# Value blocks side by side behind the whole fold, with scores and mixing in other PSUM banks

## What is computed

```python
x_c = einsum('bct,bcd->bdt', x, W[condition])                 # 128 samples, 32 tokens, 512
q_c = hidden @ Wq_c.T + bq_c                                  # 192 wide
q   = (q_c @ Wq_up.T + bq_up) -> 32 heads of 192
kv  = hidden @ Wkv_c.T + bkv_c                                # 64 latent + 64 rope
k_nope, v = (kv[..., :64] @ Wkv_up.T + bkv_up) -> 32 heads
scores = einsum('bhqd,bhkd->bhqk', q, [k_nope, k_rope]) / sqrt(192)
attn = softmax(scores, axis=-1)
o    = einsum('bhqk,bhkv->bhqv', attn, v)
out  = einsum('bhsv,Hv->bsH', o, Wo) + bo
x = x + out;  x = x + ffn(conv(x))
```

## Time and profile before

| | us |
|---|---|
| median of 3 runs | 777.69 |
| lowest, highest | 776.83, 778.36 |
| the profiled execution | 776.39 |
| its span, first to last instruction | 774.6 |
| TensorE matmuls busy in it | 752.9 |
| VectorE, ScalarE, GpSimd busy in it | 619.5, 379.4, 200.4 |

### The profile page before, as it was taken

One profiled execution on the slowest core, in us unless ns is written; L12 is line 12 of the kernel. 1 busy time (PEld: TensorE's weight loads), 2 busy tenths in 40 slices (PEclk: granted clock), 3 DMA queues, 4 the chain that ended last, 5 costly groups with the idle time before them and its releaser, 6 DMA issues.

```text
span 774.6 us, 18461 instructions
## 1 busy us (share of the span) xinstructions
PE 752.9 (97%) x7757; PEld 597.5 (77%) x7757; DVE 619.5 (80%) x1109; ACT 379.4 (49%) x675; POOL 200.4 (26%) x203
## 2 busy tenths in 40 slices
PE   9999999999999999999999999999997799999996
PEld 6777686778668767868686687778676599999996
DVE  5676899989998786777768776877889588888887
ACT  2475546546563765555454646555664322222221
POOL 4002020020002010271200000000041488888871
PEclk9999999999999999999999999999999999999999
DMA  9910010010001001001300010002207158888861
GB/s 226 243 54 5 2 58 3 1 60 2 2 2 59 2 1 29 1 3 16 84 2 2 2 55 2 1 2 58 83 2 199 55 120 216 206 204 204 203 136 69
DMA packets 42738, 51.74 MB, mean 67 GB/s; under 512 B 7024, under 2 KB 29600, under 8 KB 42656
## 3 DMA queue, kind: packets, MB, share of 16 engines
q1 hardware_dynamic: 40384, 49.87, 25.9%
q0 software_dynamic: 1056, 0.49, 0.3%
q10 hardware_dynamic: 1216, 0.19, 0.2%
HBM read 41.91 MB, written 8.63 MB: 65 GB/s over the span
## 4 chain that ended last, share of the span: by engine, by line
PE 93%; DVE 3%; ACT 2%; issue 1%; POOL 0%; DVEq 0%
PE ps L730 34%; PE ps L598 9%; PE ps L599 8%; PE ps L600 8%; PE ps L774 7%; PE ps L797 4%; PE ps L1075 4%; PE ps L1076 4%; PE ps L616 4%; PE ps L1044 2%; PE ps L693 1%; DVE z_low L1435 1%; PE ps L1032 1%; PE ps L1034 1%; PE ps L1033 1%
## 5 line engine op out<-in xcount | busy, mean ns | idle before, releaser
L1176 ACT ACTIVATE qt<-ps,m_bias 128x512 f32<-128x512 f32 x228 | 145.7, 686 | 98.7 <-PE ps L730 98.7
L730 PE MATMUL ps<-q_high,m_high 64*128 64x512 f32 x768 | 154.5, 398 | 2.0 <-ACT qt L1176 1.3
L730 PE MATMUL ps<-q_high,m_low 64*128 64x512 f32 x768 | 150.6, 388 | 0.0
L730 PE MATMUL ps<-q_low,m_high 64*128 64x512 f32 x768 | 108.2, 386 | 0.0
L1435 DVE TENSOR_TENSOR z_low<-ps,z_high 128x512 fp32r<-128x512 f32 x128 | 79.7, 683 | 17.2 <-ACT z_high L1194 15.1
L730 PEld LDWEIGHTS ps<-q_high,m_high 64*128 64x128 f32 x768 | 72.4, 184 | 24.2 <-issue 7.9
L528 POOL TENSOR_TENSOR o_sum<-o_part,o_part 128x512 f32<-128x512 f32 x7 | 9.1, 1303 | 291.8 <-ACT o_part L1204 291.8
L730 PEld LDWEIGHTS ps<-q_low,m_high 64*128 64x128 f32 x768 | 72.5, 184 | 14.9
L730 PEld LDWEIGHTS ps<-q_high,m_low 64*128 64x128 f32 x768 | 72.5, 184 | 13.8
L1194 ACT CAST z_high<-ps 128x512 fp32r<-128x512 f32 x128 | 66.7, 597 | 18.7 <-PE ps L797 9.5
L1181 ACT ACTIVATE sc<-sc 128x512 f32<-128x512 f32 x60 | 37.3, 632 | 46.6 <-DVE sc L1420 43.1
(11 more groups left out here) (292 smaller groups left out, 1647.3 us busy)
## 6 DMA issues: line engine op xcount, KB each, us to landing
x_in<-in_x SPq DMA_DIRECT2D x16, 512.0 KB, 3.6
x_s<-in_x SPq DMA_DIRECT2D x32, 256.0 KB, 5.5
out<-res SPq DMA_DIRECT2D x31, 256.0 KB, 3.3
toep_high<-taps_scratch SPq DMA_DIRECT2D x32, 192.0 KB, 4.4
toep_low<-taps_scratch SPq DMA_DIRECT2D x32, 192.0 KB, 4.9
toep_far<-taps_scratch SPq DMA_DIRECT2D x32, 64.0 KB, 5.6
wq_nope<-in_L_attn_Wq_up SPq DMA_DIRECT2D x2, 768.0 KB, 10.7
wq_nope<-in_L_attn_Wq_up SPq DMA_DIRECT2D x1, 1536.0 KB, 17.5
```

The costliest lines, as they stand in the source:

```text
L730: mm = pe.matmul(ps[:, fold_bank(u, j) + e, :], weights[rows, (GH * g + j) // 2, c, :], moving[c][rows, :], start=start, stop=stop)
L1176: act.activation(qt[:, j, :], ps[:, fold_bank(u, j) + j % 2, :], ACT.Identity, bias=m_bias[:, h:h + 1]).then_inc(s["qt_done"], 1)
```

## The change

The two value blocks now follow each other, behind all 16 heads of the fold, in units 1 to 14. Block 1 of units up to 13 goes to BT, BT + 1, BS, BS + 1, which are the fold's banks, so it waits for all heads to be taken (qt_done and qt_last), and no longer for z_low. Scores go to BZ, BZ + 1, BX, BT instead of BS, BS + 1, BX, BT: in units from 1 the four groups wait for z_low 1, 2, 3 and 5 of the unit before, where the first two waited for none; in unit 0 the first group waits for the weights' low parts (fold_done 6 and wvT_done 4), where the third waited for wvT_done 4. Mixing goes to BT + 1, BS (even) and BS + 1, BZ (odd). The waits of turn_latent, tap_products and turned_ffn(0) are turned to counters of scores taken, as their banks are now held by scores. ScalarE takes the four banks of block 0 in one go behind head 14, VectorE takes head 15 ahead of the first z_low.

```diff
-    ZBANK = ((BZ, BZ + 1, BX, BO), (BT, BT + 1, BZ, BZ + 1))
+    ZBANK = ((BZ, BZ + 1, BX, BO), (BT, BT + 1, BS, BS + 1))
-    SBANK = (BS, BS + 1, BX, BT)
+    SBANK = (BZ, BZ + 1, BX, BT)
-    MIX_BANK = lambda i, e: (BS + e if i % 2 else BT + e if i == 0 else (BT + 1, BZ)[e])
+    MIX_BANK = lambda i, e: (BS + e if i == 1 else BT + e if i == 0 else ((BT + 1, BS), (BS + 1, BZ))[i % 2][e])
...
                 elif i >= 2:
-                    pe.wait_ge(s["s_taken"], 4 * (i - 2) + 2)
+                    pe.wait_ge(s["zl_done"], 8 * (i - 2))
+                    pe.wait_ge(s["s_taken"], 4 * (i - 2) + 1)
...
                 if k == 0:
                     pe.wait_ge(s["fold_done"], QUADS - 2)
-                else:
-                    pe.wait_ge(s["zl_done"], 16 * k)
+                pe.wait_ge(s["s_taken"], 8 * k + 2)
...
-                if n == 2:
-                    if u == 0:
-                        pe.wait_ge(s["wvT_done"], 4)
-                    else:
-                        pe.wait_ge(s["zl_done"], 8 * (u - 1) + 3)
-                if n == 3 and u >= 1:
-                    pe.wait_ge(s["zl_done"], 8 * (u - 1) + 5)
+                if u >= 1:
+                    pe.wait_ge(s["zl_done"], 8 * (u - 1) + (1, 2, 3, 5)[n])
+                elif n == 0:
+                    pe.wait_ge(s["fold_done"], QUADS - 2)
+                    pe.wait_ge(s["wvT_done"], 4)
...
-                        pe.wait_ge(s["qt_done"], qt_count(v, GH - 2))
-                        pe.wait_ge(s["qt_last"], 2 * v - 1)
-                        pe.wait_ge(s["zl_done"], 8 * u + 2)
+                        pe.wait_ge(s["qt_done"], qt_count(v, GH))
+                        pe.wait_ge(s["qt_last"], 2 * v)
...
                     fold(u, 8, 16)
-                    values(0, 0)
-                    scores(1, 0)
-                    scores(1, 1)
-                    values(0, 1)
-                    scores(1, 2)
-                    scores(1, 3)
                 else:
-                    fold(u, 0, 14)
-                    values(u - 1, 0)
-                    fold(u, 14, 16)
-                    values(u - 1, 1)
-                    for n in range(4):
-                        scores(u, n)
+                    fold(u, 0, 16)
+                values(u - 1, 0)
+                values(u - 1, 1)
+                for n in range(4):
+                    scores(u, n)
...
-                    values(u - 1, 0, 0, 3)
                     fold(u, 14, 16)
-                    values(u - 1, 0, 3, 4)
+                    values(u - 1, 0, 0, 4)
...
                 late_head(u, GH - 3)
-                if u == 1:
-                    late_head(u, GH - 1)
-                    values(0, 0, 0, 4)
-                else:
-                    values(u - 1, 0, 0, 2)
-                    late_head(u, GH - 1)
-                    values(u - 1, 0, 2, 4)
+                late_head(u, GH - 1)
+                values(u - 1, 0, 0, 4)
```

More of the change, by code:

```diff
@@ L874, in tap_products @@
                 pe.wait_ge(s["gf_ready"], 1)
-                if n == 0:
-                    pe.wait_ge(s["zl_done"], 64)
-                else:
-                    pe.wait_ge(s["s_taken"], 4 * 8 + 3)
+                pe.wait_ge(s["s_taken"], 4 * 8 + (1, 3)[n])
                 for h in range(16 * n, 16 * n + 16):
@@ L886, in turned_ffn @@
                 if k == 0:
-                    pe.wait_ge(s["zl_done"], 8 * (LAST - 1))
+                    pe.wait_ge(s["s_taken"], 4 * (LAST - 1) + 1)
                 if k == 1:
```

## The result

| | before | after |
|---|---|---|
| median, us (20 runs each) | 775.81 | 779.06 |
| lowest, highest | 773.93, 778.36 | 775.64, 780.67 |
| the profiled execution, us | 776.39 | 780.49 |
| its span, us | 774.6 | 778.7 |
| mean granted TensorE clock in it | 0.998 | 0.993 |

The ratio is 1.0037, 95% interval 1.0025 to 1.0049: slower by 0.37%, some 2.9 us (the plain difference of the two medians is 3.3). The median lies within 0.3 us of the forecast and inside its range, but the kernel before came out 1.9 us lower in this larger set of runs than in the three that the forecast started from. So the difference is 2.9 us and not 1.1, and that the median came so near is luck: the start was taken 1.9 us too high and the difference 1.8 us too small, and the two cancel. The outcome is "slower by over 0.2%", which had 41%, not "within 0.2%", which had 46% and was the forecast.

A forecast was written before the change was run, and what follows sets the result against it. TensorE's stream was taken to bound the kernel. The terms +2.0 - 0.88 + 1.24 - 1.04 - 0.21 gave +1.1 us; 777.69 stood 1.3 under the forecast of 778.8 us, range 776.8 to 781.0.

The forecast's parts named there:

- What bounds the kernel: TensorE, busy 752.9 of 774.6 us; time moves only where its own stream gets shorter or longer.
- The ordinary unit: Units 2 to 8, 10 to 13, start of block 0 (V) to output: 8.28 us, 0.18 longer each, +2.0 together.
- Unit 1: Its end, where scores were split around block 1 and waited three times: -0.88 us.
- unit 0: Its first scores group newly waits for all four value weights, wvT_done 4: +1.24 us.
- unit 14: Its end, 8.49 us because of unpacked weights, goes to 8.28 as the z chain starts later: -0.21 us.
- Block 1's wait for both late heads: Block 1's new wait at unit ends is covered by block 0's 1.13 us, with 0.1 us over.
- Unit 9: Its end, 9.32 us from ScalarE's late z_high, goes to 8.28: -1.04 us, or 0 if the stall stays.
- Rival 4: A stall like that in unit 9 stays on the ScalarE and VectorE path: +2.1 us, 779.8; 15%.
- Rival 3: Fourth (and second) score groups wait as z_low runs slower, 0.17 us in 13 units: +3.3 us, 781.0; 20%.
- Rival 2: Drains at tiling changes decide, first z_low not late, every unit's end at 7.87 us: -4.2 us, 773.5; 12%.
- The LAST unit's code is the same: From the LAST unit to the end nothing changes: 0 us.
- What follows in a unit: Scores are taken from 0.5 us behind the output's start; turned latents and second mixing stay covered, no new wait.

The follow-up runs named there:

- the longer wait: The changed kernel with unit ends' first scores group waiting for the second z_low instead of the first; 788.41 us, 1.0136 of before.
- filled: Matmuls without a reader added in TensorE's waits of the tail, to either kernel: 775.64 and 774.43 us for before, 777.22 and 776.92 for changed.
- the padded kernel: The kernel before with seven idle matmuls of 512 columns ahead of unit 3's fold; 778.94 us against 778.03, ratio 1.0008.

## Why the prediction was right, and where it missed

**What bounds the kernel** was right: TensorE's stream, and the first z_low as the thing that ends the wait in each unit. **The ordinary unit** came out step by step: the pair 2.0 us (2.04), V + 1.24 and V + 1.86 unchanged, scores at V + 2.67 (2.67), output at V + 6.27 (6.24). The blocks' matmuls end at V + 2.19, so TensorE stands 0.51 (forecast 0.41, with the blocks ending at V + 2.26 at the latest); the sum is the same, since the z_low ends the wait in either case. The waiting is shown by making it longer (0.60 more gave 0.60 more).

**Unit 1** (-0.85 for -0.88), **unit 0** (+1.21 for +1.24) and **unit 14** (-0.21) were right; for the first two the experiments took or gave back just that. Block 1's wait for both late heads was covered, except in unit 1, where block 1 stands 0.67 us behind block 0's loads. The scores would have waited for the z_low until V + 2.67 in any case and start at V + 2.79, so this costs 0.1 (V to output 6.36 for 6.27).

**Unit 9, the step that failed within the sum.** I wrote that its stall "would be spent before anything needs ScalarE" and took -1.04. But it isn't tied to ScalarE's place in the stream, nor to ScalarE. In the changed kernel (weight loads, then ScalarE, then SyncE):

```profile
369.57 2.57 PEld L795 LDWEIGHTS ps<-pT,ctok 32*64 32x64 f32 x128 [0.35 <-issue]
372.31 0.14 PEld L772 LDWEIGHTS ps<-qt,kv 128*32 128x32 f32 x5 [0.17 <-issue]
...
376.33 0.19 PEld L598 LDWEIGHTS ps<-z_high,wvT_high 128*128 128x128 f32 x1 [0.84 <-DVE z_low L1421]
```

```profile
370.82 4.25 ACT L1181 CAST z_high<-ps 128x512 fp32r<-128x512 f32 x8 [0.45 <-PE ps L795]
```

```profile
365.55 2.30 SPq L380 DMA_DIRECT2D taps_scratch<-o_sum  x3
```

Here ScalarE is on time, at V + 1.25, but TensorE's own 128 loads stretch from 1.95 to 2.57, and its scores' stretch is longer too. Before, it was ScalarE that was late: in all six profiles with the old order the loads of block 0 take their 0.96, and z_high starts at V + 1.46 to V + 2.33 instead of 1.24, with block 1's loads halted as well in the kernel before (1.22 instead of 0.96). In the six with the new order z_high starts at V + 1.25 to 1.61, and TensorE's loads are halted. In the seventh, with the longer wait, both are late (z_high at V + 2.04, loads in three pieces). V to output was 6.76 to 7.53 in these six, where the ordinary units have 6.27, and 8.69 to 9.32 in the old six, where they have 8.11. So the stall hits unit 9 in either order, on ScalarE's side in the old one and mostly on TensorE's in the new, and moving ScalarE's work didn't spend it. Rival 4 was right in this, and its +2.1 is the nearest to what was measured, though it put the stall in ScalarE's and VectorE's chain. So unit 9 changed by -0.56, +0.09 and +0.34 in three pairs of profiles instead of -1.04. In each profile three stores of the convolution's taps are issued by SyncE 2.4 to 4.6 us ahead of V, loads of x behind them, and the DMA engines are 0.8 busy or more in a part of unit 9's end (0.92 from 370 to 372 us here). That these transfers cause the stall is argued from the coincidence; no kernel moved them, and it stays **open**.

**Rival 3** did not occur: eight z_low take 4.87, which is 0.60 from one to the next, and the fourth score group didn't wait. **Rival 2** needed scores that don't wait for z_low; they wait 0.51 us in each ordinary unit.

**The tail, the step that failed outside the sum.** "The LAST unit's code is the same" was taken to mean that its time is. Its instructions are; their clock isn't. In the first pair 2.6 of 4.1 us arose there. That this is the clock and not the changed banks is shown by the tails above: filled, both kernels take the same, and unfilled their length goes with the time at the lower level. The shift alone didn't bring it in the padded kernel, and over the runs the loss is in both kernels. Of the 20 runs of the changed kernel two had a mean clock of 1.0 (775.64 and 776.12) and the other eighteen 0.991 to 0.996 (777.85 to 780.67). Between the filled kernels the change costs 1.6 and 2.5 us on two chips, 0.2 to 0.3%; between the kernels as they are, 2.9 and 2.3 by the ratios. From the first fold to V of unit LAST, the three profiles with the whole old order take 544.2 to 544.7 us and the four with the whole new one 546.3 to 547.1, 2.3 apart in the mean. So the forecast's +1.1 was low by some 1.2 in the structure, of which unit 9 is 1.0 in the mean (0.5 to 1.4) and the fold stretches the rest; the tail came on top in the first comparison. Whether the change makes a dip more likely: on the one chip where both kernels' clocks are on record side by side it doesn't; for the first chip, where the clocks of the kernel before are not on record, it stays **open**.

**What follows in a unit** was right: the scores are taken from 0.38 behind the output's start (forecast 0.5), with nobody late.

## What to carry to other kernels

Before a block that covers a chain on other engines is moved, work out when the chain's first result is seen, from rows of its start, its duration and the release. Here the two halts that side-by-side blocks save were worth less than the cover: by the forecast 0.23 against 0.41 us, and measured some 0.17 us a unit were lost. Where only one unit has no cover to lose (unit 1 here), make the change there alone, which kept the gain of 0.9 us and none of the cost. When a difference of a few tenths of a per cent is to be explained, compare the granted clock by stretches first, and remove the idle time that lets it fall from both kernels: that gave a cleaner comparison, and was itself worth about as much as the change cost (2.4 and 1.25 us on two chips, against 1.6 and 2.5).

## What the runs showed of the hardware

- The granted clock of TensorE went to the lower level behind idle times of 3.2 and 2.0 us in an otherwise busy stream, for 3.4 or 6.8 us, and not in every execution of the same code. It also fell in unit 9 of the kernel with the longer wait, to 0.54 of full speed in 378 to 380 us, behind the halted loads and an idle time of 1.20 us. Filled with matmuls without a reader, the places of the tail kept 1.00 in all seven profiles, and the median fell by 0.14 to 0.31% for the kernel before.
- TensorE's weight loads of a values block can be halted with nothing to wait for: 128 loads took 2.57 instead of 1.95 us, and in the second profile of the changed kernel they came in pieces, with idle times of 0.34, 0.24 and 0.20 put down to issue:

```profile
369.87 1.61 PEld L795 LDWEIGHTS ps<-pT,ctok 32*64 32x64 f32 x98 [0.35 <-issue]
371.81 0.63 PEld L795 LDWEIGHTS ps<-pT,ctok 32*64 32x64 f32 x12 [0.34 <-issue]
372.67 0.21 PEld L795 LDWEIGHTS ps<-pT,ctok 32*64 32x64 f32 x5 [0.24 <-issue]
373.09 0.29 PEld L795 LDWEIGHTS ps<-pT,ctok 32*64 32x64 f32 x13 [0.20 <-issue]
```

- The start of the first fold varied between 31.4 and 34.0 us over executions of nearly the same code, as much as the whole effect of this change.
